# A four-layer stack on one core: interleaved state updates, spread in column groups, a new order of pieces, another attention stage

## The chip, the cores and the metric

One NeuronCore of a Trainium2 chip runs the whole program in one launch. The metric is the device time of that launch in microseconds. Engines are named as the profile names them: PE (TensorE), PEld (its weight loads), DVE (VectorE), ACT (ScalarE), POOL (GpSimd) and SP (SyncE, which issues most DMAs).

## The reference

Input x has 4 batches of 512 positions and 512 channels in float32. Three recurrent layers of one form come first. Cut to what matters:

```python
# layers 0..2: 32 heads of 16 channels
xa = layer_norm(x); sx = shift(xa) - xa
xxx = tanh((xa + sx*maa_x) @ maa_w1) -> five streams through maa_w2
xk, xw, xv, xr, xg = xa + sx*(maa + xxx)
w = exp(-exp(time_decay + tanh(xw @ td_w1) @ td_w2))
r, k, v, g = xr @ Wr.T, xk @ Wk.T, xv @ Wv.T, silu(xg @ Wg.T)
for each position:                    # per head, state s is 16 x 16
    a = outer(k, v); out = r @ (u*a + s); s = a + w*s
x = x + (group_norm(out) * g) @ Wo.T
xc = layer_norm(x) and shift as above -> xk2, xr2
x = x + sigmoid(xr2 @ Wfr.T) * (square(relu(xk2 @ Wfk.T)) @ Wfv.T)
# layer 3: attention, 16 heads of 32, over 1024 context rows with a mask
a = layer_norm(context)
p = softmax(mask(Q(x) @ K(a).T * 32**-0.5))
x = x + tanh(gate) * ((p @ V(a)) @ Wo.T)
```

## The kernel before

**Layers.** The sequence is cut in two halves of 256 positions. A unit is one batch and one half of one layer, 24 in all. Positions of a unit are taken in leaves of 8: products within a leaf are made in three levels on VectorE with head sums on TensorE (`products`, L715, tiles P0a to P4d). The state at the start of each leaf comes from a scan over 32 leaves (`scan`, L1527), and `outputs` (L761) adds the part of the state to each position's output. The addends of the scan are the state updates: `updates` (L740) makes, for one pair of channel blocks and one quarter `q` of the leaves' rows, 16 matmuls of 32 x 32 x 128 columns, all from the same 32 rows `32*q` of `k_t` and `v_m`, into the four column groups `g` of one PSUM bank. There are two pairs and four quarters, so eight tiles a unit. ScalarE copies each tile into the scan's input (`update`, L1131).

A layer norm takes four pieces on TensorE (`norm`, L612): column sums s1, their spread m1, quarter sums s2, and i1, where `spread` (L607) sends the inverse deviations of 64 positions in each of four rows to all partitions. A unit has two norms: norm A before the streams, norm C before the feed part. Each matmul written on float32 data is two instructions for TensorE, a transpose is one.

Three units are in work at once in step `s`: unit e = s-2 in its feed part, c = s-1 in its output product and norm C, b = s in its recurrence, and n = s+1 in norm A and the streams. The order of the pieces is written out by hand, once for each engine: TensorE's list begins at L800, ScalarE's at L1183, VectorE's at L1595. PSUM banks are handed out in rings (`Ring`): a tile waits until the tile that had its bank before it is emptied. Ring A (norm A, lora, streams) has banks 0 to 2, ring B (products, by-token turns, updates, turned norms) banks 3 and 4, ring O bank 5, ring C banks 6 and 7. The lists `A_TILES`, `B_TILES`, `C_TILES` hold each ring's order. SP's queue has the loads and stores of x, and `load_vm`, which sets up `v_m` for the updates. The big weights come through POOL's queue in three slots.

**Attention.** Four batches, each with 16 blocks: 4 channel groups of 4 heads, times 4 blocks of 128 positions. For each head `scores` (L960) makes 128 x 1024 scores in two banks; VectorE adds the mask and takes the maximum (L1734); ScalarE takes the exponential and its sum (L1310); `turned` (L970) transposes the 128 x 1024 probabilities in eight pieces against the identity (L976). ScalarE and VectorE copy four pieces each (L1303, L1739). `weighted` (L979) first turns the inverse sums of the block (L985), then multiplies by the values (L994); VectorE scales the result (L1752). Scores run `LAG = 3` heads ahead of `turned`. The loop over all 256 heads is written out straight, over batch boundaries. A table `BESIDE` says behind which head each other tile stands: the projections of K and Q for later channel groups, the output product of the batch before, and the normalisation of the context, first projections and values of the next batch (`mean`, `var`, `rstd`, `k00`, `k01`, `q0`, `v0` to `v7`). Only the first batch's are made ahead of the heads (`FIRST`).

```python
BESIDE = {... (10, 2): [(1, "mean0"), (1, "mean1")], (11, 1): [(1, "var")], ...
for n in range(HEADS + LAG + 1):
    if n < HEADS:
        scores(n)
    if n % HPT == HPT - 1 and n >= HPT:
        weighted(n // HPT - 1)
    if 0 <= n - LAG < HEADS:
        turned(n - LAG)
    for b, name in beside(n):
        batch_tile(b, name)
```

K and Q are split in two float32r parts and laid side by side by SP: 32 DMAs a channel group (L543, L548). SP also loads context (L509), x (L518) and mask (L514), and stores the result in quarters (L553).

Of the kernel before, what the change touches and what calls it, by code (L numbers as in the profile page):

```python
# [13 lines left out]
P = 128  # L14
# [43 lines left out]
GROUPS = B * KT  # L58
BLOCKS = GROUPS * TT
HEADS = BLOCKS * HPT  # L60
Q_PART, K_PART = (0, 0, 1, 1), (0, 1, 0, 1)
LAG = 3
X_STORED = 16 * ITS

BESIDE = {(0, 2): [(0, "k10")], (1, 0): [(0, "k11")], (1, 2): [(-1, "wo0")], (2, 0): [(-1, "wo1")], (2, 2): [(0, "q1")], (3, 0): [(-1, "wo2")],
# [4 lines left out]
FIRST = ["mean0", "mean1", "var", "rstd0", "rstd1", "k00", "k01", "q0"] + [f"v{n}" for n in range(ST)]  # L74
PARTS = [f"{w}{e}{n}" for e in range(KT) for w, n in (("k", 0), ("k", 1), ("q", ""))]


def beside(n):
    if not 0 <= n < HEADS:
        return []  # L80
    b, u, h = n // (TT * KT * HPT), n // HPT % (TT * KT), n % HPT
    return [(b + off, name) for off, name in BESIDE.get((u, h), ()) if 0 <= b + off < B]


def turned_tiles():
    tiles = [(0, "var", "act")]
    for n in range(HEADS + LAG + 1):
        tiles += [(n // HPT - 1, "rb", "act")] if n % HPT == HPT - 1 and n >= HPT else []
        tiles += [(n - LAG, "t", "act")] if 0 <= n - LAG < HEADS else []
        tiles += [(b, name, "act") for b, name in beside(n) if name == "var"]  # L90
    return tiles


def other_tiles():
    def of(b, name):
        return [] if name == "var" else [(b, name, "act" if name[0] == "v" else "dve")]

    tiles = []
    for name in FIRST:
        tiles += of(0, name)  # L100
    for n in range(HEADS + LAG + 1):
        tiles += [(n // HPT - 1, "out", "dve")] if n % HPT == HPT - 1 and n >= HPT else []
        tiles += [(n - LAG, "t", "dve")] if 0 <= n - LAG < HEADS else []
        for b, name in beside(n):
            tiles += of(b, name)
    return tiles + [(B - 1, f"wo{m}", "dve") for m in range(KT)]

# [3 lines left out]
           ("w2w1", "dve"), ("w2v1", "dve"), ("w2k1", "dve"), ("v0", "act"), ("td1", "act"), ("v1", "act"), ("td2_0", "act"), ("td2_1",  # L111
           "act"), ("w2r0", "dve"), ("w2g0", "dve"), ("k0", "act"), ("w2r1", "dve"), ("w2g1", "dve"), ("k1", "act"), ("r0", "act"), ("r1",
           "act"), ("g0", "act"), ("g1", "act")]
B_TILES = [("P0a", "dve"), ("P0b", "dve"), ("VT0", "act"), ("VT1", "act"), ("P1", "dve"), ("P2a", "dve"), ("P2b", "dve"), ("P4a", "dve"),
# [24 lines left out]
def laid_out():  # L139
# [15 lines left out]
    for i, name in enumerate(("th", "thg", "tdh", "st_a")):  # L155
# [5 lines left out]


RW_AT, RW_COLS = laid_out()


AT_AT = {"mbias": (448, SK), "wk": (1600, SLOT), "mask": (3648, SK // 4), "probs_t": (4000, 4096), "wo": (8096, SLOT), "an": (10144, 4096),
         "wv": (14320, SLOT), "wq": (16368, SLOT), "vals": (18416, ST * 384), "vals3": (21488, 2 * ST * P), "k_part": (23536, 2 * SK), "q_part": (25584, 2 * T),
# [1710 lines left out]
```

## Time and profile before

| | us |
|---|---|
| median of 3 runs (lowest to highest) | 3555.29 (3549.32 to 3556.19) |
| the profiled execution | 3555.04 |
| its span | 3553.2 |
| PE busy | 3326.4 (94%) |
| PEld busy | 2507.2 (71%) |
| DVE busy | 2632.3 (74%) |
| ACT busy | 1861.2 (52%) |
| POOL busy | 109.9 (3%) |

The mean granted clock of TensorE is 0.968 of full speed. The span is from the first to the last instruction of the core; the time has 1.8 us more around it. "Idle before" in a group is time in which the engine stood still ahead of such an instruction, with what ended it. The chain of waits follows the work that ended last back to what released it; a piece "x16" is 16 instructions in a row.

### The profile page before, as it was taken

To read this page: it belongs to the slowest core of one execution; us is meant where nothing else is said; L and a number is where in the kernel's file an instruction comes from. 1 tells how busy PE (TensorE), PEld (TensorE's weight loads), DVE (VectorE), ACT (ScalarE), POOL (GpSimd) and SP (SyncE) were. 2 spreads that over 40 slices of the span, in tenths; PEclk is the share of its full clock that TensorE was granted. 3 is DMA by queue.
4 is the path that set the end of the run, shared out by engine and by line. 5 is a ranking of instruction groups with operands and counts; after the bars stand their busy time and mean duration, and the time that the engine had idled before them with its cause. 6 is when DMAs were issued, how large, how long until landed. Compare 5 with 4: busy or idle time off the path is not lost.

```text
span 3553.2 us, 74824 instructions
## 1 busy us (share of the span) xinstructions
PE 3326.4 (94%) x31856; PEld 2507.2 (71%) x31856; DVE 2632.3 (74%) x3721; ACT 1861.2 (52%) x3087; POOL 109.9 (3%) x204
## 2 busy tenths in 40 slices
PE   6899999999999999999999999996697997997998
PEld 4667777778787777777878777775355565665666
DVE  3788888888888888888888888875155565465566
ACT  2455554555555555555555555443155555555555
POOL 1000000000000000000000000000000000000000
PEclk9899999999999999999999999998799999999999
DMA  3113332232333333233233223222324133132221
GB/s 119 60 67 108 108 120 96 105 134 91 107 117 108 108 108 109 102 123 120 90 108 116 97 108 120 94 97 78 110 54 107 48 75 94 37 84 85 60 70 51
DMA packets 91914, 336.65 MB, mean 95 GB/s; under 512 B 16704, under 2 KB 37824, under 8 KB 65600
## 3 DMA queue, kind: packets, MB, share of 16 engines
q0 software_dynamic: 27648, 201.34, 15.7%
q1 hardware_dynamic: 63936, 130.52, 12.6%
q8 instruction: 255, 4.18, 0.5%
q14 instruction: 75, 0.61, 0.1%
HBM read 252.11 MB, written 16.78 MB: 76 GB/s over the span
## 4 chain that ended last, share of the span: by engine, by line
PE 86%; DVE 6%; ACT 3%; SPq 2%; DMA 2%; issue 1%; POOL 0%; ACTq 0%; DVEq 0%; POOLq 0%
PE psum L704 39%; PE psum L713 5%; PE psum L773 5%; PE psum L750 4%; PE psum L976 4%; PE psum L952 3%; PE psum L942 3%; PE psum L994 3%; PE psum L966 2%; SPq L548 2%; PE psum L957 2%; PE psum L948 2%; PE psum L659 2%; DVE psum L1734 1%; PE psum L669 1%; PE psum L609 1%
## 5 line engine op out<-in xcount | busy, mean ns | idle before, releaser
L704 PE MATMUL psum<-rw 128*128 128x256 f32 x6144 | 1421.7, 388 | 19.5 <-DVE rw L1435 10.6
L704 PEld LDWEIGHTS psum<-rw 128*128 128x128 f32 x6144 | 1172.8, 194 | 234.5 <-issue 52.8
L1547 DVE TENSOR_TENSOR rw<-rw 128x2048 f32<-128x2048 f32 x192 | 429.5, 2279 | 18.7 <-ACT rw L1151 16.7
L1734 DVE CUSTOM_DVE_ANT_0 psum<-psum,mem 128x1024 f32<-128x1024 f32 x256 | 313.5, 1225 | 114.1 <-PE psum L966 114.0
L1310 ACT ACTIVATE rest<-psum,mem 128x1024 f32<-128x1024 f32 x256 | 284.9, 1113 | 72.7 <-DVE mem L1734 70.8
L976 PE MATMUL psum<-ident,rest 128*128 128x128 f32 x2048 | 272.7, 276 | 3.9 <-DVE mem L1704 3.8
L976 PEld LDWEIGHTS psum<-ident,rest 128*128 128x128 f32 x2048 | 236.7, 142 | 44.2 <-issue 13.5
L1096 ACT ACTIVATE rw<-psum 128x512 f32<-128x512 f32 x192 | 111.5, 593 | 297.3 <-PE psum L704 297.1
L1429 DVE SCALAR_TENSOR_TENSOR rw<-psum,rw 128x256 f32<-128x256 f32 x480 | 196.4, 477 | 72.6 <-PE psum L659 52.8
L1034 ACT ACTIVATE rw<-rw 128x256 f32<-128x256 f32 x192 | 99.8, 590 | 273.5 <-DVE rw L1379 273.5
L966 PE MATMUL psum<-side 128*128 128x512 f32 x512 | 212.3, 496 | 30.5 <-ACT rest L1310 22.6
L1303 ACT ACTIVATE mem<-psum 128x512 f32<-128x512 f32 x256 | 151.8, 593 | 159.3 <-PE psum L976 159.3
L713 PE MATMUL psum<-rw 128*128 128x512 f32 x432 | 220.7, 612 | 14.4 <-DVE rw L1517 8.4
L1530 DVE TENSOR_TENSOR_SCAN rw<-rw 128x2112 f32<-128x2112 f32 x48 | 218.7, 4556 | 16.5 <-ACT rw L1134 16.5
L1134 ACT ACTIVATE rw<-psum 128x512 f32<-128x512 f32 x192 | 197.7, 1141 | 28.5 <-PE psum L750 28.4
L773 PE MATMUL psum<-rw 128*32 128x128 f32 x6144 | 200.2, 277 | 6.1 <-DVE rw L1547 6.1
L1739 DVE COPY mem<-psum 128x512 f32<-128x512 f32 x256 | 176.0, 687 | 35.6 <-PE psum L976 35.4
L1151 ACT ACTIVATE rw<-rw 128x1024 f32<-128x1024 f32 x96 | 191.6, 2070 | 0.0
L773 PEld LDWEIGHTS psum<-rw 128*32 128x32 f32 x6144 | 161.4, 111 | 37.8 <-issue 17.4
L750 PE MATMUL psum<-rw 32*32 32x128 f32 x6144 | 180.8, 274 | 1.2 <-ACT rw L1134 1.2
L1812 POOL DMA_DIRECT2D rw<-big_dram x192 | 101.5, 529 | 2355.0 <-PE psum L704 2342.5
L750 PEld LDWEIGHTS psum<-rw 32*32 32x32 f32 x6144 | 142.0, 105 | 41.4 <-issue 39.1
(149 smaller groups left out, 4389.7 us busy)
## 6 DMA issues: line engine op xcount, KB each, us to landing
rw<-big_dram POOLq DMA_DIRECT2D x192, 1024.0 KB, 5.1
side<-mem SPq DMA_DIRECT2D x256, 128.0 KB, 2.4
rw<-xs_dram SPq DMA_DIRECT2D x32, 512.0 KB, 3.3
side<-mem SPq DMA_DIRECT2D x256, 64.0 KB, 2.0
rw<-rw SPq DMA_DIRECT2D x192, 64.0 KB, 1.9
xs_dram<-rw SPq DMA_DIRECT2D x24, 512.0 KB, 2.7
rw<-x_dram SPq DMA_DIRECT2D x16, 512.0 KB, 3.3
mem<-ctx_dram SPq DMA_DIRECT2D x4, 2048.0 KB, 8.1
```

The lines of the kernel that those rows point to most:

```text
L704: last = mm(t[:, o * TC:(o + 1) * TC], big[:, k, P * m:P * m + P], src[:, k, 0:TC], start=k == 0, stop=k == KT - 1, skip_group_check=True)
L713: b_ring.fill(mm(t, blk, src, start=True, stop=True), it, name)
L750: last = mm(t[32 * g:32 * g + 32, k, :, :, s], k_t[rows, s, 256 * pair + at:256 * pair + at + 32], v_m[rows, s, :, at:at + 32], start=True ...
L773: last = mm(t[32 * q:32 * q + 32, o, s, :], rz[:, k, c, 32 * m:32 * m + 32], s_bd[:, half, NM * i + m, :], start=False, stop=c == 3, skip_ ...
L966: last = mm(t[:, sh, :], q_side[group % 2][:, h, P * q:P * q + P].bitcast(F32R), k_side[group % 2][:, h, sh * 512:sh * 512 + 512].bitcast( ...
L976: last = nc.tensor.transpose(tokens(t, o), tokens(probs[:, n % HPT, :], first + o), ident[:])
L1134: b_ring.empty(f(to, t, ACT.Copy), it, f"U{pair}{q}")
L1310: s_ring.empty(f(probs[:, n % HPT, :].rearrange("p (a s) -> p a s", a=2), s_ring.bank(n, "s"), ACT.Exp, scale=-1.0, bias=mx[:, n % 8:n % 8 ...
L1429: last = stt(to[:, m, :], t[:, o * TC:(o + 1) * TC], par(layer, MAAS, KT * FAN[s] + m), sxa[:, m, :], ALU.add, ALU.mult)
L1530: state_dve.inc(nc.vector.tensor_tensor_scan(s_flat, d_flat, s_flat, 0.0, ALU.mult, ALU.add), it, f"scan{pair}")
L1547: state_dve.inc(tt(s_bd[:, half, :, :].rearrange("p c (h j) -> p c h j", h=4), own, place, ALU.mult), it, f"b{k}{half}")
L1734: maxima.inc(nc.vector.tensor_tensor_reduce(t, t, mbias.rearrange("p (a s) -> p a s", a=2), 1.0, 3.4e38, ALU.add, ALU.min, accum_out=mx[:, ...
```

## The change

In the layers:

- `updates` takes two quarters at a time, in two row groups and two banks, and issues their matmuls in turns. Count and data stay.
- `spread` makes each of its four matmuls as four, one for each column group of 32.
- The order of pieces on TensorE, ScalarE and VectorE changes, and with it the order of the rings.

In the attention:

- The straight loop over 256 heads becomes a loop of four turns (one for each batch) with register values in waits; each turn begins with the batch's normalisation, first projections and values and ends with its output product. `BESIDE`, `LAG` and the second set of values go.
- A step has a block's scores in turns with the transposes of the block before; the weighted values of the block two back stand behind the step's first scores.
- The probabilities are turned by a plain matmul against a diagonal matrix of the inverse sums, in place of a transpose against the identity and a scaling at the end. VectorE makes the diagonal, and negates each maximum in an instruction of its own.
- Value tiles are copied by VectorE, no longer by ScalarE. Probabilities have two buffers. The result of a batch is stored by one DMA.

The diff, cut to its core:

```diff
             def spread(t, src):
                 for q in range(4):
-                    last = mm(t[:, 64 * q:64 * q + 64], pick[:, q, :], src, start=True, stop=True, skip_group_check=True)
+                    for g in range(4):
+                        last = mm(t[32 * g:32 * g + 32, 64 * q:64 * q + 64], pick[:, q, 32 * g:32 * g + 32], src, start=True, stop=True, skip_group_check=True)
...
-            def updates(it, pair, q):
-                if q == 0:
+            def updates(it, pair, n):
+
+                if n == 0:
                     pe.wait_ge(vm_loaded, 16 * 4 * (2 * it + pair + 1))
                     pe.wait_ge(*b_ring.empty_at(it, "KT1"))
...
+                two = (2 * n, 2 * n + 1)
+                t = [opened(b_ring, it, f"U{pair}{q}").rearrange("p (k j c s) -> p k c j s", k=2, j=32, c=4) for q in two]
...
                         for g in range(4):
                             at = 32 * g + P * k
...
+                            for i, q in enumerate(two):
+                                rows = slice(32 * q, 32 * q + 32)
+                                last[i] = mm(t[i][32 * g:32 * g + 32, k, :, :, s], k_t[rows, s, 256 * pair + at:256 * pair + at + 32], v_m[rows, s, :, at:at + 32],
+                                             start=True, stop=True, skip_group_check=True)
```

TensorE's new list of a step, in the code's names (a pair of updates is `updates(b, pair, n)`):

```
fr0, s1 A, values by token, fk0, P0a, P0b, m1 A, P1, P2a, fr1, P2b, s2 A, wo0, i1 A, fk1, wo1, P4a, P4b,
lora, P4c, P4d, keys by token, lora_three 0, updates(0,0), own outputs 0, s1 C, lora_three 1, updates(0,1),
fv0, decay_in, fv1, decay_out, updates(1,0), v0, m1 C, outputs 00, lora_two 0, v1, outputs 01, updates(1,1),
s2 C, lora_two 1, outputs 10 11, k0, k1, own outputs 1, r0, i1 C, outputs 20 21, r1, outputs 30 31,
turned norm 0, g0, g1, turned norm 1
```

TensorE's new attention loop:

```diff
+            with pe.Fori(0, B) as b:
...
+                def transposed(u, h):
+
+                    if h == 0:
+                        pe.wait_ge(diag_ready.sem, diag_ready.at(b, u + 1))
+                    for n, (t, full) in enumerate(((tile_a(A_T + HPT * u + h), a_full), (None, d_full))):
+                        if n == 1:
+                            t = tile_d(D_AT["t", u, h])
+                        for o in range(4):
+                            st = 4 * n + o
+                            last = mm(t[:, P * o:P * o + P], probs[u % 2][:, h, P * st:P * st + P], diag[:, h, :], start=True, stop=True, skip_group_check=True)
+                        full.inc(last)
...
+                for step in range(UNITS + 2):
+                    for h in range(HPT):
+                        if step < UNITS:
+                            scores(step, h)
+                        if h == 0 and step >= 2:
+                            weighted(step - 2)
+                        if 1 <= step <= UNITS:
+                            transposed(step - 1, h)
+                    for tile in projected(step):
+                        project_tile(tile)
```

`projected` gives the two K tiles of group j+1 in the first two steps of group j, and Q of group j+2 in the second. A batch's head on TensorE is mean 0 and 1, q0, the variance, q1, rstd 0 and 1, k00, k01, v0 to v7. SP issues the next context and mask behind the side loads of the last group of the batch.

## Rows read from the trace of the kernel before

**Rows 1.** The page, span in 40 slices, busy tenths.

```profile
PE   6899999999999999999999999996697997997998
DVE  3788888888888888888888888875155565465566
```

**Rows 2.** Busy time by window: us, then PE, PEld, DVE, ACT, POOL, PEclk, DMA.

```profile
1487.30:1585.70 98.40, 98.33 (x1008) 78.06 (x1007) 85.04 (x112) 54.52 (x87) 4.23 (x9) 1.00 0.35 130
...
600.00:1580.00 980.00, 979.36 (x10022) 777.91 (x10021) 843.54 (x1099) 539.01 (x859) 41.18 (x78) 0.99 0.30 108
```

**Rows 3.** Chain of waits in the layers, 1480 to 1590 us: start, us, what.

```profile
1498.51 1.49 PE psum L750 x64
...
1501.20 1.54 PE psum L750 x61
...
1509.85 1.01 PE psum L750 x32
...
1518.18 1.09 PE psum L693 x16
...
1523.36 3.65 PE psum L704 x16
...
1529.08 0.45 PE psum L604 x32
...
1539.82 1.04 PE psum L609 x8
1540.86 3.51 PE psum L704 x16
...
1571.06 0.58 PE psum L604 x32
...
1576.15 0.84 PE psum L609 x8
```

**Rows 4.** The chain where the attention begins.

```profile
2527.86 9.53 PE psum L931 x16
...
2568.21 27.48 PE psum L952 x64
...
2631.92 0.59 SPq L548
```

**Rows 5.** The chain in later blocks: four in the first batch, two in the last.

```profile
2649.51 0.47 PE psum L966 x2
...
2651.97 1.02 PE psum L976 x8
...
2656.95 0.87 PE psum L976 x8
2657.82 3.44 PE psum L942 x8
...
2663.72 1.02 PE psum L976 x8
...
3479.51 1.95 PE psum L994 x64
...
3488.94 1.95 PE psum L994 x64
```

**Rows 6.** Groups, costliest first: busy us, mean ns, idle before and its releaser.

```profile
L704 PE MATMUL psum<-rw 128*128 128x256 f32 x6144 | 1421.7, 388 | 19.5 <-DVE rw L1435 10.6
...
L1734 DVE CUSTOM_DVE_ANT_0 psum<-psum,mem 128x1024 f32<-128x1024 f32 x256 | 313.5, 1225 | 114.1 <-PE psum L966 114.0
L1310 ACT ACTIVATE rest<-psum,mem 128x1024 f32<-128x1024 f32 x256 | 284.9, 1113 | 72.7 <-DVE mem L1734 70.8
...
L1303 ACT ACTIVATE mem<-psum 128x512 f32<-128x512 f32 x256 | 151.8, 593 | 159.3 <-PE psum L976 159.3
```

**Rows 7.** Waits of PE in the attention: us in total, times, longest.

```profile
PE psum L931 <- DMA mem<-ctx_dram: 36.4, 3, 12.4
```

**Rows 8.** Groups of the attention alone, the smallest VectorE work of a block.

```profile
L1743 DVE RECIPROCAL mem<-mem 128x4 f32<-128x4 f32 x64 | 10.8, 169 | 0.0
```

More of the change, by code:

```diff
@@ L78, in beside @@
[L78 to L91, printed above, removed]
@@ L94, in other_tiles, with projected @@
[L94 to L106, printed above, removed]
+def projected(step):
+    j, part = step // TT, step % TT
+    tiles = [("k", j + 1, part)] if part < 2 and j + 1 < KT else []
+    return tiles + ([("q", j + 2)] if part == 1 and j + 2 < KT else [])
@@ L960, in scores @@
-            def scores(n):
-                b, group, q, h = head(n)
-                if q == 0 and h == 0:
-                    pe.wait_ge(side_loaded[group % 2], side_at(group))
-                t = opened(s_ring, n, "s")
-                for sh in range(2):
-                    last = mm(t[:, sh, :], q_side[group % 2][:, h, P * q:P * q + P].bitcast(F32R), k_side[group % 2][:, h, sh * 512:sh * 512 + 512].bitcast(F32R),
-                              start=True, stop=True)
-                s_ring.fill(last, n, "s")
@@ L997, in _ @@
[L997 to L1010 removed]
+                    d_full.inc(last)
@@ new lines, in scores @@
+                def scores(u, h):
+                    e, q = u // TT, u % TT
+                    if q == 0 and h == 0:
+                        pe.wait_ge(side_loaded[e % 2], sides(b, e))
+                    pe.wait_ge(s_free.sem, s_free.at(b, HPT * u + h + 1 - 2))
+                    t = banks_s(HPT * u + h)
+                    for sh in range(2):
+                        last = mm(t[:, sh, :], q_side[e % 2][:, h, P * q:P * q + P].bitcast(F32R), k_side[e % 2][:, h, sh * 512:sh * 512 + 512].bitcast(F32R),
+                                  start=True, stop=True)
+                    s_full.inc(last)
@@ new lines, in weighted @@
+                def weighted(u):
+                    pe.wait_ge(a_free.sem, a_free.at(b, A_T + HPT * u + HPT))
+                    t = tile_d(D_AT["out", u])
+                    pe.wait_ge(d_free.sem, d_free.at(b, D_AT["t", u, HPT - 1] + 1))
+                    e = u // TT
+                    for st in range(ST):
+                        for h in range(HPT):
+                            last = mm(t[AD * h:AD * h + AD, 0:P], vals[:, st, (HPT * e + h) * AD:(HPT * e + h + 1) * AD], probs_t[:, st, h, :],
+                                      start=st == 0, stop=st == ST - 1, skip_group_check=True)
+                    d_full.inc(last)
@@ L1012, in _ @@
+                for m in range(KT):
+                    t = tile_d(D_AT["wo", m])
+                    for k in range(KT):
+                        last = mm(t, wo[:, k, P * m:P * m + P], ao[:, k, :], start=k == 0, stop=k == KT - 1)
+                    d_full.inc(last)
+                for c in (a_full, d_full, s_full):
+                    c.close()
         @block.scalar
```

809 lines of the change are left out of this document (355 added, 454 removed), and 4 rows, old and new, of the table BESIDE.

## The prediction

> **What bounds the kernel now.** I read the page first. Its strip of slices shows two stages: up to slice 28 TensorE is at nine tenths and VectorE at eight, then both dip and VectorE stays about six [rows 1]. The first stage is the recurrent layers (24 units), the second, from 2527.9 us, the attention. Then busy time by window: in the layers TensorE is busy 979.4 of 980 us, VectorE 843.5; one unit takes 98.4 us, and VectorE works 85.0 of them [rows 2]. So a microsecond of TensorE taken out of a unit comes back, up to about 13. The chain of waits over one unit gives the price of its pieces [rows 3], the chain at the start of the attention what its first batch costs [rows 4], the chain further on the steady blocks [rows 5], and the groups and waits what the other engines do [rows 6 to 8]. A block of four heads takes 11.75 us (2651.97 to 2663.72) with one projection tile of 3.44 in it, so 8.3 without; where no tile is left it takes 9.43 (3479.51 to 3488.94) [rows 5]. TensorE and VectorE are nearly level there.
>
> **The sum's base.** The profiled execution took 3555.0 us (span 3553.2, 1.8 around it), the median of the three runs is 3555.3: the same for this purpose. About 0.2% (7 us) is the least that a measurement of this kernel tells from no change.
>
> **Layers, state updates.** A unit has eight update tiles of 32 instructions. The first two pairs take 1.49 and 1.54 us, the other four tiles stand alone at 1.01 (one of the four rows is shown): 7.05 in all [rows 3]. The change issues each pair as one run of 64 that alternates between two row groups and two banks. Row groups alone overlap nearly fully: a tile of the decay stream, two groups of 64 rows, takes 1.09 us for 16 instructions, 68 ns each, against 109 for a transpose of as many columns on the full array (0.87/8 [rows 5]). Column groups alone come down to 14 ns an instruction (32 in 0.45, at 64 columns) [rows 3]. Both together are not in the trace. Low end: 64 x 14 ns = 0.90, plus 0.15 to enter the mode (1.02 against 0.87 [rows 5]), 1.05 a run. High end: 1.5, today's pair. I take 1.05, as the stream of 128 columns in eight tiles at once is that of 64 columns in four, the 14 ns row: 4 x 1.05 = 4.2, a gain of 2.85 a unit (1.05 at the other end).
> The Trainium skill, "TensorE: Matmul & The Clock Gate", section "Back-to-back issue gap", says that start to start never drops below about 25 ns. By that a run would be 1.6 us and a unit would gain 0.65. The trace differs, with its 14 ns.
>
> **Layers, spread.** Eight instructions with 128 columns of weights become 32 in four column groups. They cost 0.84 (norm A) and 1.04 (norm C); the shape they get costs 0.58 when entered from another mode and 0.45 in its own, and the full-array tile behind it then takes 3.65 in place of 3.51 [rows 3]. Norm A: 0.84 + 3.51 - 0.58 - 3.65 = 0.12. Norm C, now ahead of output blocks of the same mode: 1.04 + 3.51 - 0.45 - 3.65 = 0.45. Together 0.57 a unit.
>
> **Layers, order.** No work is added; by my count of both lists the mode changes stay the same (32 and 33). I walked VectorE's new list against TensorE's. Three places lose cover. Keys by token follow P4c and P4d directly, without a feed tile between, and need their banks emptied by VectorE: 0.3. The second pair of updates needs two ScalarE copies of 1.0 that stand behind the scan inputs: 0.25. The g stream waits for a mix that VectorE makes after block 31: up to 0.6. Part of it hides; I take 0.4, ends 0 and 2. VectorE's 85 us stay below the 95 that remain. Layers: (2.85 + 0.57 - 0.4) x 24 = 73 us less; ends 85 less and 10 more.
>
> **Attention, which the diff replaces too.** (a) Turning: eight transposes a head, one instruction each, 0.87 us [rows 5], become eight plain float32 matmuls against a diagonal of inverse sums. A plain one is two instructions: a unit's four streams, output product and three feed products make 128 matmuls, over 24 units 3072, and the group has 6144 [rows 6]. Each streams 256 columns in 219 ns (3.51/16), as a transpose streams 128 in 109. So a head takes 16 x 109 ns = 1.74, 0.87 more, on the path.
> A block is then scores 4 x 0.47, turning 4 x 1.74, entry 0.15, weighted values 1.95: 10.9 us. VectorE's block fits in today's 8.3; it gains a diagonal of 512 columns (0.7, as its other passes of that size), loses a copy of 0.2 and gains four negations of one column. These aren't in the trace: at most 0.17 each (the reciprocal of four columns [rows 8]), at least nothing; I take 0.12. 9.3 in all, hidden by TensorE; if a block of TensorE fell below that, it would be the bound.
> (b) Order. Scores ran three heads ahead; now the weighted values of a block follow the first scores of the next but one. From the end of a step's fourth scores: maximum 1.3, negation 0.2, exponential 1.3, ScalarE's copy 0.6 = 3.4 [rows 6]; TensorE arrives after 1.74 + 0.47 = 2.2 and waits 1.2. In six of sixteen steps a projection covers it: 10 x 1.2 = 12 a batch.
> (c) Batches. Normalisation, projections and values of the next batch lay among the heads; now each batch starts with them. In today's first batch the stretch from the first mean to the last value tile is 67.8 us (2527.86 to 2595.69), 2.6 of it for cold means (9.53 against 2 x 3.44) [rows 4]. The new stretch has one projection more, 3.4, and two that fill waits, about 5 of their 6.9. That makes 64 a warm batch; 51 of it is TensorE's work, 13 are idle.
> (d) What goes: the wait for the context at three batches, 36.4 us [rows 7], as that load is issued a third of a batch earlier; and the turned inverse sums, 0.1 a block. SP's side loads stay: 32 issues of 0.59 and 3 to land, 22 us, covered at a batch's start by the value tiles, 27.5 [rows 4].
> Per batch: 64 + 16 x 10.9 + 12 + 3.5 (a first step of scores alone) + 8 x 3.44 + 2 (the last two steps) + 4 x 3.44 = 297; four are 1188. Add 2.6 for the cold start, 3 for one store of 1 MB at the end in place of a last quarter, 4 for the loop: 1198 against today's 1025.3, so 173 more. The loop's jumps and its waits on register values are not in the trace: nothing at the low end, 77 at the high (three waits a head at 0.1, the largest gap of pure issue that I count); I take the low end, since each engine's queue runs ahead. Ends of the whole: waits hidden and a stretch of 58, 105 more; clock and register waits, 250 more.
> Sum: 3555 - 73 + 173 = **3655 us**.
>
> **Rivals.** *The updates don't speed up* (0.17). 1.49/64 is 23.3 ns an instruction; if that is a limit of issue and not of the stream, only the merging gains, 1.05 a unit: layers 29 less, 3699. For it: today's pairs already cross two row groups and gain little. Against: the 14 ns row. The skill's 25 ns is this rival's rule.
> *More waits in the attention* (0.17). Waits on registers at 0.05 each, 12 a block, 38 us, and after the gaps at a batch's start the half clock, under which the first means took 9.53 in place of 6.9 [rows 4], for some 8 us a batch: 70 more, 3725.
> *The turning costs nothing* (0.04), the other side. If a plain matmul of 128 columns took what a transpose takes, the turning of each head would be 0.87 and a block VectorE's 9.3; that and the hidden waits give 64 x 1.6 + 40 = 142 less, 3513. It decides once a head's turning is below about 1.2 us. The two instructions speak against it.
> *The turning costs four times* (0.02): a head 3.5 us, 256 x 1.74 above my sum, 4100. The skill's page "TensorE: Matmul & The Clock Gate", section "Terms", calls transpose mode 4 times faster for FP32; the rows give 2.
>
> **Numbers.** Forecast 0.60, by itself 3610 to 3695. With the first two rivals the range is 3605 to 3745; outside it are the turning's rivals and orders that gain or lose more than my ends. Faster 0.04, same 0.02, slower 0.94.
>
> **What would show it.** Layers: the update line at about 1.05 us for 64, a unit near 95.4, TensorE busy throughout. Attention: 4096 turning instructions at 109 ns, blocks of 11 to 12 us, four stretches of some 64 us with VectorE half idle. Wrong if a head turns in 0.9 us, if TensorE waits several us a unit for VectorE, or if batch starts stay hidden.

## The result, and the profile of the changed kernel

The changed kernel takes **3729.73 us** (median of four runs, 3728.78 to 3730.11) against 3552.31 (3547.9 to 3556.19) for the kernel before: ratio 1.0499, 95% interval 1.0481 to 1.0518. It is slower, as forecast, and inside the range of 3605 to 3745. But it is 75 us above the 3655 of the sum and outside the 3610 to 3695 of the forecast by itself; it is in the range only because the rivals widened it. The profiled span is 3728.3 us.

The page of the changed kernel: totals, and the strip of slices that answers to [rows 1].

```profile
PE 3461.5 (93%) x34992; PEld 2654.3 (71%) x34992; DVE 2766.0 (74%) x4009; ACT 1857.4 (50%) x2984; POOL 109.9 (3%) x204
...
PE   6899999999999999999999999868998998998998
...
DVE  3788888888888888888888888714673673675575
```

VectorE's strip shows four dips, one at the start of each batch of the attention. Nothing in the strip tells that the layers missed their gain.

**Where the stages end.** The first means of the attention begin at 2508.53 and the span ends at 3728.3: 1219.8 us, where the sum had 1198 and the kernel before 1025.3. The wait for the first context, which follows on the layers' last store, begins at 2492.8, and in the kernel before at 2512.4. So the layers gained 20 where I had 73 (53 short), and the attention lost 194 where I had 173 (22 more): together the 75.

**The layers.** The first scan of the third unit and of the 23rd, in VectorE's timeline of the kernel before (start, us):

```profile
317.43 4.56 DVE L1530 TENSOR_TENSOR_SCAN rw<-rw 128x2112 f32<-128x2112 f32 x1
...
2300.85 4.55 DVE L1530 TENSOR_TENSOR_SCAN rw<-rw 128x2112 f32<-128x2112 f32 x1
```

And of the changed kernel:

```profile
318.04 4.55 DVE L1476 TENSOR_TENSOR_SCAN rw<-rw 128x2112 f32<-128x2112 f32 x1
...
2276.57 4.55 DVE L1476 TENSOR_TENSOR_SCAN rw<-rw 128x2112 f32<-128x2112 f32 x1
```

Twenty units take 1983.42 us before and 1958.53 after: **99.17 and 97.93 a unit**, a gain of 1.24. The sum had a unit of 98.4 going to 95.4. This measure of a unit is used for every run below.

Busy time by window, of the changed kernel, for the stretches of [rows 2] (a unit is now 97.95 long):

```profile
600.00:1580.00 980.00, 960.12 (x10543) 746.91 (x10543) 854.02 (x1112) 556.10 (x880) 42.21 (x80) 1.00 0.31 111
1487.30:1585.25 97.95, 96.08 (x1057) 74.80 (x1060) 85.37 (x111) 55.88 (x89) 4.22 (x8) 1.00 0.34 122
```

TensorE was busy 979.4 of 980 us before; now it is idle for 19.9 of them. VectorE works the same 85 us a unit. The waits of PE between 300 and 2300 us name what TensorE waits for (us in total, times, longest); the same view of the kernel before has no line at all:

```profile
PE psum L628 <- DVE rw L1375: 9.9, 21, 0.5
PE psum L673 <- ACT rw L1079: 9.3, 21, 0.4
PE psum L673 <- DVE rw L1381: 7.5, 17, 0.5
PE psum L638 <- ACT rw L1061: 6.4, 21, 0.3
```

Four waits of a third to half a microsecond, once in nearly every unit. The chain of waits over one unit shows that they are links of one ring:

```profile
1488.32 1.71 DVE rw L1375 x5
...
1493.01 4.48 DVE rw L1476
...
1497.73 1.11 ACT rw L1134
...
1506.16 0.59 ACT rw L1079
...
1506.89 3.71 PE psum L673 x16
...
1516.10 4.46 DVE rw L1476
...
1529.67 4.49 DVE rw L1493 x2
...
1535.15 1.15 DVE rw L1381
...
1536.34 7.17 PE psum L673 x32
...
1564.86 0.58 PE psum L578 x32
...
1579.79 0.70 DVE rw L1463
```

From 1536.34, where the g stream starts, to 1579.77 TensorE works alone, 43.4 us without a gap. From there to the next g stream, 54.4 us, the chain runs mainly over VectorE and ScalarE: values of P4d (L1463), the mixtures from the lora (L1375), the first scan (L1476), the states turned by ScalarE (L1134), the decays' exponentials (L1061), ScalarE's copy of v0 (L1079), the stream v1, the second scan, the spread of the states over their blocks (L1493), and the mixture g (L1381), for which the g stream waits. Short TensorE pieces, some 7 us together, lie in that second stretch too (half of the keys by token, the second lora matmuls in two groups, v1). The ring closes once a unit: 43.4 + 54.4 = 97.8. I call it **the loop** below.

**The pieces themselves came out as priced.** Timeline of TensorE in the same unit; L723 are the state updates:

```profile
1498.73 1.16 PE L723 MATMUL psum<-rw 32*32 32x128 f32 x64
```

A run of 64 takes 1.09 us start to start (1499.82 - 1498.73), where I took 1.05; the spread (L578) takes 0.58 when entered.

**The attention.** Groups of the changed kernel (busy us, mean ns, idle before and its releaser):

```profile
L960 PE MATMUL psum<-mem 128*128 128x128 f32 x4096 | 502.6, 276 | 0.0
...
L971 PE MATMUL psum<-mem 128*32 128x128 f32 x4096 | 125.1, 274 | 54.9 <-ACT mem L1293 51.7
```

Its chain over the start of the second batch, and its first blocks (L960 turns the probabilities, L971 are the weighted values):

```profile
2813.53 6.87 PE psum L898 x16
...
2876.92 0.48 PE psum L947 x2
...
2905.92 1.98 PE psum L960 x16
...
2908.37 1.78 PE psum L960 x16
...
2915.77 0.49 ACT mem L1293
...
2916.48 1.95 PE psum L971 x64
```

The head of a batch takes 63.4 us (2813.53 to 2876.92) where I had 64. The turning of a head takes 1.78, and 1.98 behind the weighted values, where I had 1.74. The weighted values wait for ScalarE's exponential and copy, 51.7 us in 37 places where I had 48 in 40. The third batch begins at 3116.8: a batch takes 303.3, not 297. The granted clock falls to its lower level in each batch's head: summed over windows of 2 us, it lacks 26.6 us of full clock in the changed kernel's attention, where it lacked 41.6 in that of the kernel before.

### The profile page after: what moved, and what is told of

Same layout as the page of the kernel before. It is cut to its first block, busy times and chain, and to the rows that moved or that the text cites. A ratio compares the mean times of both kernels' runs of the same rounds, so it can differ in the third digit from the quotient of the medians.

```text
span 3728.3 us, 83232 instructions
## 1 busy us (share of the span) xinstructions
PE 3461.5 (93%) x34992; PEld 2654.3 (71%) x34992; DVE 2766.0 (74%) x4009; ACT 1857.4 (50%) x2984; POOL 109.9 (3%) x204
## 4 chain that ended last, share of the span: by engine, by line
PE 62%; DVE 24%; ACT 6%; issue 5%; SPq 2%; DMA 1%; POOL 0%; ACTq 0%; DVEq 0%; POOLq 0%
PE psum L673 23%; PE psum L960 10%; DVE rw L1493 6%; DVE rw L1476 5%; PE psum L682 5%; DVE rw L1375 5%; PE psum L906 3%; PE psum L971 3%; PE psum L935 3%; PE psum L947 3%; DVE rw L1381 2%; ACT rw L1134 2%; PE psum L908 2%; PE psum L990 2%; PE psum L628 1%
## 5 line engine op out<-in xcount | busy, mean ns | idle before, releaser
L673 PEld LDWEIGHTS psum<-rw 128*128 128x128 f32 x6144 | 1155.3, 192 | 232.0 <-issue 54.1
L960 PEld LDWEIGHTS psum<-mem 128*128 128x128 f32 x4096 | 490.0, 191 | 26.9 <-issue 11.9
L960 PE MATMUL psum<-mem 128*128 128x128 f32 x4096 | 502.6, 276 | 0.0
L1288 ACT ACTIVATE mem<-psum,mem 128x1024 f32<-128x1024 f32 x256 | 285.2, 1114 | 433.7 <-DVE mem L1689 433.7
L1493 DVE TENSOR_TENSOR rw<-rw 128x2048 f32<-128x2048 f32 x192 | 432.8, 2285 | 5.3 <-ACT rw L1134 3.5
L1375 DVE SCALAR_TENSOR_TENSOR rw<-psum,rw 128x256 f32<-128x256 f32 x480 | 196.8, 477 | 101.8 <-PE psum L628 50.7
L1476 DVE TENSOR_TENSOR_SCAN rw<-rw 128x2112 f32<-128x2112 f32 x48 | 218.4, 4550 | 9.8 <-ACT rw L1117 9.8
L1117 ACT ACTIVATE rw<-psum 128x512 f32<-128x512 f32 x192 | 196.9, 1132 | 47.7 <-PE psum L723 47.6
L682 PE MATMUL psum<-rw 128*128 128x512 f32 x432 | 211.5, 608 | 8.6 <-DVE rw L1453 5.6
L947 PE MATMUL psum<-side 128*128 128x512 f32 x512 | 190.6, 454 | 17.8 <-ACT mem L1288 14.5
L1134 ACT ACTIVATE rw<-rw 128x1024 f32<-128x1024 f32 x96 | 190.3, 2037 | 0.0
L1463 DVE TENSOR_TENSOR rw<-psum,rw 128x512 f32<-128x512 f32 x168 | 115.8, 690 | 91.0 <-PE psum L682 91.0
L971 PE MATMUL psum<-mem 128*32 128x128 f32 x4096 | 125.1, 274 | 54.9 <-ACT mem L1293 51.7
L971 PEld LDWEIGHTS psum<-mem 128*32 128x32 f32 x4096 | 108.1, 110 | 78.8 <-issue 75.0
```

Of the source, the lines that this page charges most:

```text
L673: last = mm(t[:, o * TC:(o + 1) * TC], big[:, k, P * m:P * m + P], src[:, k, 0:TC], start=k == 0, stop=k == KT - 1, skip_group_check=True)
L682: b_ring.fill(mm(t, blk, src, start=True, stop=True), it, name)
L947: last = mm(t[:, sh, :], q_side[e % 2][:, h, P * q:P * q + P].bitcast(F32R), k_side[e % 2][:, h, sh * 512:sh * 512 + 512].bitcast(F32R), s ...
L960: last = mm(t[:, P * o:P * o + P], probs[u % 2][:, h, P * st:P * st + P], diag[:, h, :], start=True, stop=True, skip_group_check=True)
L971: last = mm(t[AD * h:AD * h + AD, 0:P], vals[:, st, (HPT * e + h) * AD:(HPT * e + h + 1) * AD], probs_t[:, st, h, :], start=st == 0, stop= ...
L1134: state_act.inc(f(to, s_in[:, k % 2, :, 0:NC], ACT.Copy), it, f"t{k}")
```

## The experiments

Each kernel has the kernel before beside it on the same chip; "unit" is the mean of twenty as above. Where two runs come from different comparisons I set their ratios beside each other, since the median of the kernel before lay between 3552.6 and 3556.3 there; the interval of a ratio is about 0.0015 to either side, 5 us (0.0021 for the last of the layers' runs).

### The two stages apart

The new layers, and the attention of before.

> The change's layers with the attention of before. Layers and attention don't overlap, so both theories give the layers' share of the change: the layers ended 20 us earlier in the changed profile, so about 3533 (20 below before). If the two stages interact (weights, tables, buffers), it would differ from this by more than 5.

Measured 3532.17, ratio 0.9931 (0.9916 to 0.9945), a unit of 98.01. The layers give 24 back, within the 5 us of what they gave in the changed profile, so the stages do not disturb each other by more than the runs can tell. The attention takes the rest: 194 in the profile, some 200 by the ratios. This kernel beats both, and the next ones are built on it.

### Is it the order?

The order of before with the paired updates and the spread in column groups:

```diff
-                    last = mm(t[:, 64 * q:64 * q + 64], pick[:, q, :], src, start=True, stop=True, skip_group_check=True)
+                    for g in range(4):
+                        last = mm(t[32 * g:32 * g + 32, 64 * q:64 * q + 64], pick[:, q, 32 * g:32 * g + 32], src, start=True, stop=True, skip_group_check=True)
...
-                    updates(b, 0, 2)
-                    updates(b, 0, 3)
+                    updates(b, 0, 1)
```

> Before, with only the paired updates and the spread in column groups, in the old order of pieces. Theory (the new order ate the gain): TensorE never waits in the old order, so the whole 3.1 to 3.4 us a unit come back, 75 to 82 us, about 3475. Rival (the pieces don't pay in place, or VectorE becomes the bound at once whatever the order): 20 to 30 us, about 3525.

Measured 3545.97, ratio 0.9970 (0.9959 to 0.9981), a unit of 98.94. So the new order did not eat a gain that the old one would have kept: in the old order the same edits bring still less. The waits of PE, 300 to 2300 us, of this run say why:

```profile
PE psum L670 <- ACT rw L1079: 20.6, 20, 1.1
PE psum L755 <- ACT rw L1135: 12.1, 21, 0.6
PE psum L660 <- DVE rw L1430: 9.9, 21, 0.5
PE psum L705 <- DVE rw L1436: 4.1, 20, 0.2
```

46.7 us over some 21 units, 2.2 a unit: as soon as TensorE is quicker it stands behind ScalarE and VectorE in this order too. A second thing takes a share here. Timeline of TensorE in this run, and below it busy time by window (the column before the last two is the granted clock):

```profile
1500.82 1.14 PE L755 MATMUL psum<-rw 32*32 32x128 f32 x64 [0.58 <-ACT rw L1135]
1501.89 8.86 PE L705 MATMUL psum<-rw 128*128 128x256 f32 x32
```

```profile
1502.00:1504.00 2.00, 2.00 (x5) 1.64 (x6) 2.00 (x4) 2.00 (x2) 0.00 (x0) 0.50 0.12 42
```

Right behind a cluster of updates and lora pieces with two waits in it, the clock stands at its lower level (0.50 is 1.2 GHz), and the feed and value streams that follow take 8.86 us, not 7.17. I summed what the granted clock lacks of full over all windows of 2 us between 600 and 2300 us: 30.7 us in this run, 15.4 in the kernel before (in eight places), nothing in the changed kernel. That is 1.8 us a unit here and 0.9 before. Take waits and clock off this unit: 98.94 - 2.2 - 1.8 = 94.9, which is the sum's 98.4 - 2.85 - 0.57 = 94.98. So TensorE's work did shrink about as priced, and nearly all of it went elsewhere.

The reverse: the new order, with the updates quarter by quarter and the spread in full-width pieces.

```diff
-                    for g in range(4):
-                        last = mm(t[32 * g:32 * g + 32, 64 * q:64 * q + 64], pick[:, q, 32 * g:32 * g + 32], src, start=True, stop=True, skip_group_check=True)
+                    last = mm(t[:, 64 * q:64 * q + 64], pick[:, q, :], src, start=True, stop=True, skip_group_check=True)
...
+                for i, q in enumerate(two):
+                    rows = slice(32 * q, 32 * q + 32)
+                    for k in range(2):
...
```

> The new order with the old spread and the updates one quarter after the other, attention of before. Theory (the cycle binds): of the old pieces only the update pair between the two lora parts and norm A's i1 lie on the cycle, so 0.5 to 1 us a unit more than e1, about 3550 to 3560. Rival (TensorE's work bound): all 3.0 us a unit more than e1, about 3605.

Measured 3545.44, ratio 0.9968 (0.9958 to 0.9977), a unit of 98.36, and PE waits for the other engines 0.5 us in all. The clock lacks nothing between 600 and 2300 us. This is not quite the order alone, since all four pairs of updates now stand together. Timeline of TensorE in this run:

```profile
1494.98 1.56 PE L754 MATMUL psum<-rw 32*32 32x128 f32 x64
```

A pair takes 1.49 us in its chain of waits, as today's pairs do, so the updates take 5.96 a unit and no longer 7.05. The run gains 11 us in all, 0.81 a unit. The clock gives 0.9 of that and the merged pairs 1.1, so the new order costs some 1.2 us a unit in other places; 0.4 of it is a pause behind P4d that is read below, and the rest was not found. On top of it the two edits of TensorE's work give 13 more: 0.35 us a unit, and 4 us where the pipeline of units fills (the third unit's scan starts at 317.64 and not at 322.06). Yet they take some 2.2 us of TensorE's work out of a unit, 1.6 of the updates (1.49 to 1.09 a pair) and 0.57 of the spread. TensorE was all but full at 98.36 (busy for 98.06 of it), and just below, at 98.0, the loop takes over.

### Where the loop can be cut

P4c moved ahead of the lora, in the hope that P4d and with it the mixtures would come sooner:

```diff
+                    products(b, "P4c")
...
-                    products(b, "P4c")
```

> e1_layers_only with one product tile, P4c, moved ahead of lora on TensorE. Theory (a unit is a cycle: TensorE alone from the g stream to P4d, then VectorE and ScalarE from P4d to the mix of g): P4d then ends 0.9 us earlier after lora and keys by token wait less, 1.2 us a unit, 29 less than e1, about 3504. Rival (VectorE's busy time and scattered waits bound the unit): within 5 of e1.

Measured 3541.44, ratio 0.9958 (0.9943 to 0.9973), a unit of 98.19. A miss for both theories: it is 9 us slower than the kernel that it was made from, where one had 29 less and the other at most 5 of difference. P4c stays inside the 43 us in which the loop runs over TensorE, so that stretch is as long as it was, and a fifth wait (for the values of P4c, 7.3 us in 21 places) comes on top.

Two cuts of VectorE's work. The first leaves out half of the feed's output; the second, half of the decays of levels 1 and 2:

```diff
-                c_ring.empty(tt(gate_, gate_, t, ALU.mult), it, f"fv{n}")
+                c_ring.empty(tt(gate_[:, 0:256], gate_[:, 0:256], t[:, 0:256], ALU.mult), it, f"fv{n}")
...
-                f_dve.inc(tt(v, v, gate_, ALU.add), it, f"x{n}")
+                f_dve.inc(tt(v[:, 0:256], v[:, 0:256], gate_[:, 0:256], ALU.add), it, f"x{n}")
```

> The new layers with the attention of before, and in each unit VectorE's multiplication by the gate and the addition that close the unit (x{n}) on 256 of 512 columns; half of the feed's output is left out. This takes about 1.07 us of VectorE out of the stretch in which TensorE waits on the chain values, keys by token, second lora matmuls, mixing, scan. Theory (a loop through TensorE, VectorE and ScalarE holds the unit at 97.9 us): each unit is shorter by 1.07, x 24 = 26, so 3532 - 26 = 3506. Rival (TensorE's own work is the bound, its idle time is only what the modelled ends show): 3532, within 4.

```diff
-                leaf.inc(tt(r_right, r_right, w_left, ALU.mult), it, "u1r")
-                leaf.inc(tt(k_left, k_left, w_right, ALU.mult), it, "u1k")
+                leaf.inc(tt(r_right[:, 0:64], r_right[:, 0:64], w_left[:, 0:64], ALU.mult), it, "u1r")
+                leaf.inc(tt(k_left[:, 0:64], k_left[:, 0:64], w_right[:, 0:64], ALU.mult), it, "u1k")
...
```

> The new layers with the attention of before, and in each unit the multiplications by the decays of levels 1 and 2 (u1r, u1k, u2r, u2k) on half their columns; half of these scalings is left out. The saving on VectorE is about the same 1.1 us a unit as in the run on the closing pieces, but it lies where TensorE works without a gap. Loop theory: nothing, 3532 within 4. Rival (VectorE's total, 85.4 busy of 97.8 us a unit, sets the unit): 3532 - 26 = 3506.

Measured 3529.13, ratio 0.9928 (0.9913 to 0.9942), a unit of 97.93; and 3525.98, 0.9918 (0.9903 to 0.9933), a unit of 97.91. By the ratios these are 1 and 5 us less than with the new layers alone. Neither cut moves the unit by more than 0.1 us: VectorE's total is not the bound. (The second kernel's third unit starts 6 us sooner, 311.65 against 317.64: its gain, 2 us more than I had allowed, lies where the pipeline of units fills.) But I had expected 26 us of the first, and that was a misreading of mine. Timeline of VectorE in the kernel with the new layers only; L1584 and L1586 are the halved pieces:

```profile
1497.81 0.68 DVE L1584 TENSOR_TENSOR rw<-rw,psum 128x512 f32<-128x512 f32 x1
1498.52 0.69 DVE L1586 TENSOR_TENSOR rw<-rw 128x512 f32<-128x512 f32 x1
...
1502.04 0.69 DVE L1586 TENSOR_TENSOR rw<-rw 128x512 f32<-128x512 f32 x1
```

They fall in the time in which the chain runs over ScalarE (from 1496.8 to 1506.0 in that kernel). They are inside the span of the loop, and beside it.

So a cut of the same size, 1.14 us of VectorE, at a place on the chain. It leaves out half of the spread states of one half-quarter:

```diff
+                n_c = HALF // 2 if (k, half) == (3, 1) else HALF
-                state_dve.inc(tt(s_bd[:, half, :, :].rearrange("p c (h j) -> p c h j", h=4), own, place, ALU.mult), it, f"b{k}{half}")
+                state_dve.inc(tt(s_bd[:, half, 0:n_c, :].rearrange("p c (h j) -> p c h j", h=4), own[:, 0:n_c], place[:, 0:n_c], ALU.mult), it, f"b{k}{half}")
```

> The new layers with the attention of before, and in each unit the last of VectorE's eight multiplications that spread the state over its diagonal blocks (b31) on half its columns; half of the spread states of the fourth quarter's second half is left out. Saved: 1.14 us of VectorE a unit, as much as in the runs on the closing pieces and on the decays of the levels, but on the chain behind which TensorE sits idle: it lies between the two waits of the loop. Loop theory: the unit goes from 98.04 to about 97.2, where the run with the lora banks shows that TensorE's own work takes over; 24 x (0.8 to 1.14) = 19 to 27, so 3505 to 3513. Rival (waits on VectorE are no bound wherever they lie, only what TensorE does or opens late counts): 3526 to 3532, as in the other two.

Measured 3515.24, ratio 0.9890 (0.9874 to 0.9906), a unit of 97.25: 0.76 less, and the wait for the mixture g is gone from the list of waits. The ratio is 0.0041 below that of the new layers alone, 15 us; 24 units of 0.76 are 18. One microsecond of the same engine is worth at most 0.1 us a unit at two places (1 and 5 us of the whole, with an error of 5) and 0.76 at a third (15 us). That is the loop, shown by what it lets through.

### Cutting it without leaving anything out

Two moves: the decays' last exponential goes behind ScalarE's copy of v0, and VectorE mixes the streams r and then g one after another, with g's wait behind r's work.

```diff
                     decay_out(n)
                     stream(n, "v", 0)
+                    decay_last(n)
...
-                if n == 0:
-                    for s in streams:
+                for s in streams:
+                    if n == 0:
                         turn = STREAMS * it + ORDER.index(s)
...
-                for s in streams:
                     t = filled(a_ring, it, f"w2{s}{n}")
```

> The new layers with the attention of before and two pieces moved, with nothing left out: the last exponential of the decays goes behind ScalarE's copy of v0 (0.44 us earlier for v0), and VectorE mixes r before it waits for the buffer that g shares with v (0.8 us of work that then lies beside the wait). Loop theory: 1.2 us a unit, x 24 = 30, so 3503. Rival (TensorE's own work is the bound): 3532 within 4.

Measured 3515.95, ratio 0.9890 (0.9874 to 0.9907), a unit of 97.42; the wait for v0's copy is gone. About half of what I expected: 0.59 us a unit of the 1.2 moved. The chain now takes another way, over TensorE's pieces between the first scan and the second (v1, outputs, updates, lora), which the two moves do not shorten.

The same, with the second group's lora matmuls opening their banks one by one:

```diff
+                if n == 1:
+                    for s in "wvk":
+                        t = opened(a_ring, it, f"w2{s}{n}")
+                        rows = slice(DM * ROWS_OF[s], DM * ROWS_OF[s] + DM)
+                        for o in range(2):
...
+                        a_ring.fill(last, it, f"w2{s}{n}")
+                    return
```

> As the run with two moves, and the second group's second lora matmuls open their three banks one after another and not all three before the first matmul: on the loop 1.1 us more is freed, so by the loop theory 3503 - 26 = 3477. If the two moves gave nothing this gives nothing either (3532). If only the first bank's wait is late and the third's is not, nothing beyond the two moves (3503).

Measured **3508.14**, ratio **0.9869 (0.9854 to 0.9884)**, a unit of 97.18. It computes everything and is the fastest such version of this study, 1.3% under the kernel before and 5.9% under the changed one. Under a third of the last step's expected gain came: 8 us of 26, and 0.24 us a unit of 1.1.

Its waits still had the mixture g in 12 units of 21. The on-chain cut again, on top of it (the same part left out as above):

> The same cut of 1.14 us in the kernel with two moves and the lora banks one by one (3508), where TensorE waits for g's mixture 0.46 us in 12 units of 21 only. If the loop is gone and TensorE's own work is the bound: 3508 - 6 = 3502. If a loop through VectorE still holds the unit: 3508 - 27 = 3481.

Measured 3492.94, ratio 0.9823 (0.9802 to 0.9844), a unit of 96.62. Between the two theories: 0.56 us a unit of the 1.14 come through. The waits of PE, 300 to 2300 us, then name no engine, and in the unit from 1480 us the chain outside TensorE is one piece, the values of P4d:

```profile
PE psum L788 <- issue: 8.8, 9, 1.9
PE psum L714 <- issue: 1.7, 1, 1.7
```

```profile
1549.61 1.93 PE psum L723 x4
...
1551.56 0.70 DVE rw L1523
...
1552.31 0.66 PE psum L737 x4
```

So at about 96.6 the listed waits of the ring are gone, and the changed kernel stands 1.3 above it. One pause is left that the list does not show. Keys by token, eight transposes, stand right behind P4d; timeline of TensorE in this run, and in the kernel before:

```profile
1551.54 1.42 PE L737 MATMUL psum<-ident,rw 128*128 128x128 f32 x8
```

```profile
1495.25 1.04 PE L727 MATMUL psum<-ident,rw 128*128 128x128 f32 x8
```

The next piece starts at 1552.89 here and at 1496.21 there, so the eight take 1.35 us and not 0.96. The chain puts the whole 0.76 on VectorE, but four of the eight transposes run beside it: TensorE pauses for 0.4, not for 0.76.

### The attention

ScalarE copies a turned tile before the next exponential, not after it:

```diff
+                        if step >= 1:
+                            u = step - 1
+                            t = full_a(A_T + HPT * u + h)
+                            a_free.inc(f(probs_t[:, 0:4, h, :], t.rearrange("p (s t) -> p s t", s=4), ACT.Copy))
...
-                        if step >= 1:
-                            u = step - 1
...
```

> The changed kernel with one edit in the attention: ScalarE copies a turned tile before it takes the next exponential. Theory (the weighted values wait for the last ScalarE copy, 51.7 us over 37 waits, because that copy stands behind the exponential): the copy is done 1.4 us earlier and the wait falls to what VectorE's copy leaves, about 0.65 each; 25 to 35 us less, about 3700. Rival (the exponential comes later and holds the scores instead): no gain or a loss.

Measured 3699.05, ratio 1.0403 (1.0386 to 1.042): 31 us less than the changed kernel (34 by the ratios). The wait of the weighted values is then for VectorE's copy, and shorter. Waits of PE from 2480 us on:

```profile
PE psum L971 <- DVE mem L1697: 16.6, 40, 0.8
```

The second kernel turns the probabilities by transposes against the identity again, within the new loop; the division by the sums is left out.

```diff
-                            last = mm(t[:, P * o:P * o + P], probs[u % 2][:, h, P * st:P * st + P], diag[:, h, :], start=True, stop=True, skip_group_check=True)
+                            last = nc.tensor.transpose(t[:, P * o:P * o + P], probs[u % 2][:, h, P * st:P * st + P], ident[:])
```

> The changed kernel with the turning by a transpose against the identity; the scaling by the inverse sums is left out (the diagonal is still made). Theory (the plain matmul costs 0.9 us a head more and is on the path): the turning line falls from 4096 to 2048 instructions, a block falls from 12.5 us to VectorE's 9.3 plus 0.5 to 1, 140 to 170 less, about 3575. Rival (a transpose costs a quarter of it, as a page has it: 0.45 a head): the turning line below 0.5 us a head. Rival (VectorE's list holds the block): less than 80 us.

Measured 3647.14, ratio 1.0257 (1.024 to 1.0275): 83 less (86 by the ratios), near the rival and far under the 140 to 170 of the theory. The turning itself halves, as its instructions do. A block of four heads takes 12.5 in the changed kernel (3659.25 to 3671.76) and 12.7 or 11.1 here. Its chain where no projection is left (two blocks, then the last weighted values):

```profile
3594.48 3.06 PE psum L971 x64
...
3607.20 1.96 PE psum L971 x64
3609.16 1.04 PE psum L960 x8
...
3610.22 0.49 DVE mem L1697
...
3610.84 1.23 DVE psum L1686
...
3618.30 2.99 PE psum L971 x64
```

Scores, maximum, negation, exponential and copy of one head now stand in a row, and TensorE waits for the exponentials in 98 places, 72.8 us, against 14.5 in the changed kernel. Its waits for the weighted values rise to 67.8 us. And the clock takes a share. Busy time by window over the first 6 us of the block of 12.7:

```profile
3594.00:3600.00 6.00, 5.52 (x80) 5.00 (x81) 3.23 (x7) 2.07 (x4) 0.00 (x0) 0.72 0.01 3
```

The granted clock is 0.72 there; the weighted values take 3.06 us and the first turning behind them 1.55, where the block of 11.1 has 1.96 and 1.04 at full clock. That is the 1.6 between the two blocks. Over the attention the clock lacks 62.3 us of full here and 26.6 in the changed kernel. So up to 36 us of the 57 to 87 that are missing from the theory's gain are lost clock, an estimate that takes all of it to be on the path.

## Why the prediction was right, and where it was not

**Right: the sign and the attention.** The turning is two instructions where a transpose is one. I had 1.74 us a head for 0.87; the trace has 1.78 and 1.98, and the run with transposes 0.87 and 1.04. Of the 22 us that the attention lost beyond the sum, 16 are in this term and its entry (a block has 1.95 + 1.98 + 3 x 1.78 + 4 x 0.47 = 11.15 of TensorE's work and not 10.9; 64 blocks), and 4 in the waits for ScalarE's copies. The first step of each batch, with its projection, takes some 11 us where the sum had 7, for TensorE waits there for exponentials (14.5 us, nine times): some 15 more in four batches. The batch heads take 65.2, 63.4, 63.7 and 61.1, together 5 less than in the sum, and the 4 for the loop are not seen. That makes 26; where the other 4 come back was not followed. The sum came within 2% of the attention, partly because such errors cancel. And the waits for the context at the later batches are gone from the list, as the sum had it. The jumps and register waits of the loop, which I took at nothing and bounded at 77, do not show as a wait.
Against the Trainium skill, page "TensorE: Matmul & The Clock Gate", section "Terms", which has transpose mode four times faster for FP32, these runs show twice (0.87 against 1.78).

**Right: the updates and the spread as pieces.** 64 instructions in 1.09 us are 17 ns each, nearer to the 14 ns row than to today's 23. So the rival in which the updates don't speed up (3699) falls: its price for a run was 1.5 us.
The Trainium skill, page "TensorE: Matmul & The Clock Gate", section "Back-to-back issue gap", has about 25 ns as the issue floor, in its row for up to 64 columns; the trace disagrees, with 14 ns at 64 columns and 17 at 128.

**Wrong: the term "Layers, order".** This is the step that failed. I took it at 0.4 us a unit with ends at 0 and 2, on the ground that VectorE's 85 us stay below the 95 that remain. Measured by the same sum it is 98.4 - 2.85 - 0.57 = 94.98 to 97.93, **2.95 a unit**, beyond my high end, 61 us over 24 units more than I took.

The 2.95 are made up so: the four listed waits 1.6 (33.1 us over some 21 units), the waits without a releaser 0.2, the pause behind P4d 0.4, and 0.7 of TensorE's work beyond the 94.98. Of the four waits I had counted one, that for the mixture g (up to 0.6; it is 0.5). The keys by token behind P4d I had too (0.3; it is 0.4). The wait of the updates for ScalarE's copies, which I also counted, is not in the list; and I had not seen the other three: the second lora matmuls for the mixtures, the later ones for the decays' exponentials, and v1 for the copy of v0. And I priced each by its own lateness, as if TensorE's work were a line with gaps in it.

What I didn't ask is whether the waits follow from one another. They do: they are links of one ring that passes from TensorE through VectorE and ScalarE and back once a unit, and the ring was 97.9 long. Of TensorE's work in a unit, only what lies on the ring shortens it, that is the 43 us and the short pieces between, and the updates lie outside. "No work is added" does not hold either: the run with the order alone needs 98.36 a unit at full clock, although its merged updates save 1.1 of the 98.4. The sentence "a microsecond of TensorE taken out of a unit comes back, up to about 13" was the error: from 98.4 the loop let 0.4 of them back, not 13. VectorE's busy share says nothing on a ring in which it has to be on time.

That the ring holds the unit is shown by three cuts of about one size, two beside the chain (at most 0.1 a unit) and one on it (0.76), by the two versions that move waits, and by the order alone, where 2.2 us more of TensorE's work cost 0.35 a unit. In the last run of that section, 96.62 less the pause behind P4d (0.4) and the waits without a releaser (10.5 us over some 21 units, 0.5) leaves 95.7 of TensorE's work, 0.7 above the 94.98. In the old order the same subtraction gave 94.9, so most of the 0.7 belongs to the new order; which pieces it is, and what the waits without a releaser are, stays open. In the sum itself, the low end of the layers should be 82 less (3.42 x 24) and not 85; nothing hangs on it.

**Wrong, the other way: the unit of before.** I read 98.4 from one unit that had its full clock; the mean is 99.17, since eight of seventeen have a stretch at the lower level. The granted clock of 0.99 stood in [rows 2] and I passed over it. The changed kernel has no such stretch in the same windows, which gave 0.77 x 24 = 18 us back that were in no term. So of the 53 us missing, the term is 61, less these 18, and 10 are at the ends: the third unit's first scan comes 0.6 us later, from the first scan of the 23rd unit to the wait for the context it is 4.7 us longer, and the four units outside these twenty gain nothing beyond that, where 1.24 each had been 5.

**The rivals.** That the time lies beside the 3725 of "more waits in the attention" is chance: that rival had 70 us more in the attention, and 22 came. Its waits on registers do not show; its half clock did come, some 5 us in the second batch's head, but that head still takes 63.4, since the 64 was read from a batch whose clock was low too (0.50 between 2540 and 2558 us). "The turning costs nothing" claimed that VectorE's 9.3 would be the block; the run with transposes shows 11 to 12.7, so even then the kernel would have been slower, at 3647 and not 3513. Part of the 12.7 is lower clock, as said above. I had made there the same mistake as in the layers, of taking an engine's busy time for the length of a cycle that it is part of.

## What to carry to other kernels

When three engines hand work round in a ring once in a period, the period is at least the length of the ring, however far each engine is from full. So before a piece of the fullest engine is made cheaper, follow the chain of waits over one period and ask for each stretch whose it is: only what lies on the ring counts, and the same microsecond of the same engine was worth 15 us at one place, and 1 and 5, within the error, at two others. And see what the other engines do during a stretch that the chain gives to one: 0.76 us of VectorE behind P4d held TensorE for 0.4. Read a period as a mean over many, not from one, and take a small wait that comes once in every period for a link, not for a gap.

## What the hardware showed beyond that

- Sixty-four matmuls of 32 x 32 with 128 columns, in two row groups and two banks in turns, run at 17 ns from start to start, where one row group at a time gave 1.01 us for 32 [rows 3].
- A full stream of TensorE did not keep the clock up. In the kernel before, whose TensorE waits for nothing between 300 and 2300 us, the granted clock fell to 0.50 for some microseconds in eight places between 600 and 2300 us. In the one at 1402 us it fell behind two runs of updates with lora pieces between them, and the 32 large matmuls that follow took 8.86 us; behind the same pieces one unit later they took 7.17.
- How often it falls went with the order of the pieces: the clock lacked 30.7 us between 600 and 2300 us in the old order with the quicker updates, 15.4 in the old order with the old ones, and none in the changed kernel and in the run with the order alone. Of the other ten kernels in the new order two (the new layers only, the lora banks) lost 1.7 us in one place each, and the rest none. Why the new order nearly always keeps the clock was not tried by itself.
